# ScalarE takes norms and guards, GpSimd five head outputs, in the opening of a two-layer block

## The reference

```
q, k, v = split(norm(x) @ W_qkv.T);  q, k = elu(q) + 1, elu(k) + 1
att = q * cumsum(k * v) / (q * cumsum(k) + 1e-9)          # cumulative over the sequence, per channel
x = x + norm(att @ W_out.T * c)
gate, up = split(norm(x) @ T(w_gate_up).T)                # T: ternary in groups of 64, times mean |w|
h = silu(gate) * up
x = x + norm(rms_norm(h) @ T(w_proj).T)
```

## Time and profile before

| | us |
|---|---|
| median of 3 runs | 1160.17 (1159.6 to 1161.37) |
| the profiled execution | 1160.26 |
| its span, first to last instruction | 1158.4 |
| PE busy | 1098.9 |
| DVE busy | 772.9 |
| POOL busy | 534.2 |
| ACT busy | 442.3 |

### The profile page before, as it was taken

One profiled execution on the slowest core, in us unless ns is written; L12 is line 12 of the kernel. 1 busy time (PEld: TensorE's weight loads), 2 busy tenths in 40 slices (PEclk: granted clock), 3 DMA queues, 4 the chain that ended last, 5 costly groups with the idle time before them and its releaser, 6 DMA issues. The chain is left out here.

```text
span 1158.4 us, 14626 instructions
## 1 busy us (share of the span) xinstructions
PE 1098.9 (95%) x5376; PEld 659.5 (57%) x5376; DVE 772.9 (67%) x1224; ACT 442.3 (38%) x752; POOL 534.2 (46%) x493
## 2 busy tenths in 40 slices
PE   6997779998999999999999999999999999899997
PEld 5886355554566864468544774458644684454443
DVE  5999988985668687438872588527863488435323
ACT  3443546665522133422443234431444134333432
POOL 2548789977344343415434254415334253224323
PEclk9998889999999999999999999999999999899999
DMA  7021234200030210002100210002100010100001
GB/s 253 29 73 37 79 88 143 74 29 1 1 109 1 73 37 1 1 1 73 37 1 1 74 37 1 1 1 73 37 1 1 16 58 1 37 1 1 37 1 37
DMA packets 29079, 44.98 MB, mean 39 GB/s; under 512 B 1360, under 2 KB 9552, under 8 KB 29008
## 3 DMA queue, kind: packets, MB, share of 16 engines
q1 hardware_dynamic: 29008, 44.05, 11.7%
HBM read 34.60 MB, written 9.44 MB: 38 GB/s over the span
## 5 line engine op out<-in xcount | busy, mean ns | idle before, releaser
L540 PE MATMUL bank<-x3t,wgu_t 128*128 128x512 f16 x1536 | 351.1, 382 | 11.2 <-ACT ht L946 9.0
L540 PEld LDWEIGHTS bank<-x3t,wgu_t 128*128 128x128 bf16 x1536 | 149.1, 99 | 194.8 <-ACT ht L946 13.9
L1235 POOL TENSOR_TENSOR acc<-acc,ht 128x512 f32<-128x512 f32 x90 | 114.6, 1274 | 270.5 <-ACT ht L987 270.3
L576 PE MATMUL bank<-wproj_t,hid 128*128 128x512 bf16 x872 | 204.8, 380 | 3.3 <-ACT wproj_t L866 3.3
L1594 DVE TENSOR_TENSOR ht<-ht,bank 128x512 f32<-128x512 f32 x112 | 76.1, 679 | 159.8 <-PE bank L540 127.3
L521 PE MATMUL bank<-xnt,wqkv_hi 128*128 128x512 f32 x672 | 168.1, 392 | 0.0
L576 PEld LDWEIGHTS bank<-wproj_t,hid 128*128 128x128 f16 x872 | 85.2, 98 | 104.3 <-issue 4.5
L521 PEld LDWEIGHTS bank<-xnt,wqkv_hi 128*128 128x128 f32 x672 | 125.1, 188 | 26.0 <-issue 0.4
L1600 DVE TENSOR_TENSOR hid<-ht,hid 128x512 f16<-128x512 f32 x109 | 90.6, 831 | 66.3 <-ACT hid L974 66.3
L974 ACT ACTIVATE hid<-ht 128x512 f16<-128x512 f32 x109 | 68.5, 629 | 160.7 <-DVE ht L1594 160.7
L1181 POOL TENSOR_TENSOR tk<-tq,ts 128x512 f32<-128x512 f32 x28 | 55.0, 1965 | 136.6 <-DVE ts L1509 112.7
(11 more groups left out here) (178 smaller groups left out, 1558.2 us busy)
## 6 DMA issues: line engine op xcount, KB each, us to landing
raw_q<-in_L_ffn_w_gate_up_dram SPq DMA_DIRECT2D x32, 256.0 KB, 2.8
xn<-in_L_attn_x_dram SPq DMA_DIRECT2D x7, 1024.0 KB, 5.1
out_dram<-xn SPq DMA_DIRECT2D x7, 1024.0 KB, 8.8
x<-in_L_attn_x_dram SPq DMA_DIRECT2D x6, 1024.0 KB, 6.6
raw_q<-in_L_ffn_w_proj_dram SPq DMA_DIRECT2D x16, 256.0 KB, 2.9
raw_a<-in_L_attn_W_qkv_dram SPq DMA_DIRECT2D x4, 768.0 KB, 8.1
xn<-in_L_attn_x_dram SPq DMA_DIRECT2D x4, 256.0 KB, 3.2
raw_out<-in_L_attn_W_out_dram SPq DMA_DIRECT2D x1, 1024.0 KB, 9.7
```

Of the source, the lines that this page charges most:

```text
L540: last = pe.matmul(bank[:], wgu_t[:, k, first_row:first_row + P], x[:, part, k], start=(n == 0), stop=(n == 2 * KD - 1))
L576: last = pe.matmul(bank[:], hid_of(f, part, k)[:, t * P:(t + 1) * P], wproj_t[:, k], start=(k == 0 and part == 0), stop=(k == MT - 1 and p ...
L1235: pool.tensor_tensor(acc[:], acc[:], ht_of(f)[:, m % 2], ALU.add).then_inc(q["acc_done"], 1)
```

## The change

- **Norms and guard.** `norm_tile(0, ..)`, `norm_tile(1, ..)`, `finish_x1_tile` and `norm_x1_tile` of chunks 0 and 1 (4 tiles each) and `den_guard` of chunks 0 and 1 (8) go from POOL to ACT, as ACTIVATE Identity with pointer bias and, for norms, pointer scale. A column `eps_att` is added for the guard.
- **Head outputs.** `back_output` and `back_lo` of (0, 0), (0, 1), (0, 2), (0, 3), (1, 0) go from DVE to POOL. Those of (1, 1) to (1, 3) stay on DVE, with a wait for the one before.
- **Loads.** W_qkv and W_out come in 16 DMAs of 256 KB, eight before the wait for chunk 0's transposes and eight behind chunk 1's x, each with its own semaphore. The load of chunk 2's x goes one half earlier.
- **Squares.** `hidden_square` of m = 0 waits for `h_done` only, in all chunks; `hidden_gate` of m = 2 waits for `h_lo` of tile 0.
- **`SUMMED = 24`.** For batches from `SUMMED` on, DVE would add the parts again (`whole`) and PE would transpose the sum alone. There are 24 batches.
- **Orders.** The `start()` lists of PE, ACT, POOL and DVE are written anew.

```diff
-                if i < KD:
-                    rows = w_qkv.rearrange("(s j p) k -> p j s k", s=3, p=P)[:, i]
+                if r < NG:
+                    j, part = divmod(r, 3)
+                    rows = w_qkv[part * D + j * P:part * D + (j + 1) * P, :]
...
+                sp.dma_start(raw_a[j][:, part], rows).then_inc(raw_a_in[r], 16)
...
-            load_raw(0)
-            load_raw(1)
-            load_raw(2)
+            for r in range(0, 8):
+                load_raw(r)
             sp.wait_ge(t1_done, KD)
             sp.dma_start(xn[:], x_ch[1]).then_inc(x_loaded, 16)
-            load_raw(3)
-            load_raw(4)
+            for r in range(8, 16):
+                load_raw(r)
...
                 elif m == 2:
                     act.wait_ge(q["sq_done"], at(MT, c, 0))
-                    if f < 2:
-                        act.wait_ge(q["h_lo"], 1)
+                    act.wait_ge(q["h_lo"], at(MT, c, 0))
...
-                if f < 2 and m == 0:
-                    act.wait_ge(q["h_done"], 1)
+                if m == 0:
+                    act.wait_ge(q["h_done"], at(MT, c, 0))
                 else:
                     act.wait_ge(q["h_lo"], at(MT, c, m))
...
+            def norm_tile(c, *tiles):
+
+                for t in tiles:
+                    if t == 0:
+                        act.wait_ge(LN["1"]["nb_s"], c + 1)
+                    act.activation(xn[:, t], xn[:, t], ACT.Identity, bias=LN["1"]["nb"][:, t:t + 1],
+                                   scale=LN["1"]["rstd"][:, t:t + 1]).then_inc(xn1_ready, 1)
+
+            def den_guard(s, j):
+
+                tk = sets_of(s)[1][:, j % 2]
+                act.wait_ge(den_mul, at(KD, s, j))
+                act.activation(tk, tk, ACT.Identity, bias=eps_att[:, 0:1]).then_inc(den_ready, 1)
...
+            def back_output(s, j):
+
+                tq, tk, tr, ts = sets_of(s)
+                d = j % 2
+                pool.wait_ge(num_ready, at(KD, s, j))
+                pool.wait_ge(rec_done, at(KD, s, j))
+                pool.wait_ge(carry_done, 2 * KD * s + 2 * (j + 1))
+                pool.tensor_tensor(tr[:, d], tq[:, d], tk[:, d], ALU.mult).then_inc(att_out, 1)
```

More of the change, by code:

```diff
@@ L202, in sandwich_kernel @@
         RAW = 3
+        SUMMED = 24
         PARTS = 1
@@ L222, in sandwich_kernel @@
         setup_done = sem("setup_done")
-        raw_a_in = [sem(f"raw_a_in{i}") for i in range(KD + 1)]
+        raw_a_in = [sem(f"raw_a_in{r}") for r in range(4 * KD)]
         raw_q_in = [sem(f"raw_q_in{i}") for i in range(RAW)]
@@ L237, in sandwich_kernel @@
         q_diff = sem("q_diff")
+        q_whole = sem("q_whole")
         q_t = sem("q_t")
@@ new lines, in start @@
+                cast_half(11, 0, 1), finish_x1_tile(1, 0), hidden_gate(1, 4), put_half(6, 0), cast_half(12, 0)
+                finish_x1_tile(1, 1, 2), put_half(6, 1), hidden_square(1, 3), finish_x1_tile(1, 3), turn(6), cast_half(12, 1)
+                put_half(7, 0, 1), turn(7), cast_half(13, 0), hidden_gate(1, 5), hidden_hi(1, 4), put_half(8, 0)
+                norm_x1_tile(1, 0, 1, 2, 3), cast_half(13, 1), put_half(8, 1), x3_hi_of(1, 0, 1, 2, 3), cast_half(14, 0)
+                hidden_hi(1, 5), cast_half(14, 1), hidden_square(1, 4), hidden_gate(1, 6), hidden_square(1, 5), put_half(9, 0)
@@ L1074, in _ @@
+                split_x(3, 0, 1, 2, 3)
             start()
@@ L1396, in diff, with whole @@
                     dve.tensor_tensor(yq[:], yq[:], wb[:], ALU.subtract).then_inc(q_diff, 1)
+            def whole(*batches):
+                for b in batches:
+                    wb, yq = PLACES[b]
+                    dve.wait_ge(q_diff, b + 1)
+                    dve.tensor_tensor(yq[:], yq[:], wb[:], ALU.add).then_inc(q_whole, 1)
             def stats(which, c, src, wait):
@@ L1715, in start @@
-                scale_max(3), front_products(1, 2), scale_row(3), scale_rec(3), scale_bound(1), scale_sums(4), clip(2)
-                back_output(1, 1), diff(1), round_off(2), sum_keys(1, 2), back_lo(1, 1), x3_lo_of(0, 0, 1, 2, 3), row_shrink(1)
-                scale_max(4), scale_sums(5), feature_k(1, 3), sum_values(1, 2), diff(2), scale_rec(4), scale_max(5), carry_key(1, 2)
-                carry_value(1, 2), scale_rec(5), scale_sums(6, 7), hidden_value(0, 0), back_reciprocal(1, 2), clip(3)
@@ L1719, in start @@
-                feature_q(1, 3), clip(4), round_off(3), hidden_lo(0, 0), front_products(1, 3), hidden_value(0, 1), sum_keys(1, 3)
-                sum_values(1, 3), diff(3), round_off(4), carry_key(1, 3), carry_value(1, 3), scale_row(4), scale_max(6)
-                scale_rec(6), scale_row(5), scale_bound(2), clip(5), scale_max(7), scale_rec(7), back_reciprocal(1, 3)
-                back_output(1, 2), back_output(1, 3), back_lo(1, 2), hidden_lo(0, 1), back_lo(1, 3), round_off(5), clip(6)
-                hidden_value(0, 2), scale_sums(8), round_off(6), scale_max(8), hidden_value(0, 3), hidden_lo(0, 2), scale_rec(8)
@@ new lines, in start @@
+                back_reciprocal(1, 3), back_output(1, 3), back_lo(1, 2), diff(4), back_lo(1, 3), hidden_lo(0, 0), clip(5)
+                hidden_lo(0, 1), clip(6), round_off(5, 6), scale_sums(7), scale_max(7), scale_sums(8), scale_rec(7)
+                hidden_value(0, 2), scale_max(8), scale_sums(9), scale_row(6), diff(5), stats_tile("2", 1, 0, 1), scale_max(9)
+                scale_row(7), scale_bound(3), hidden_lo(0, 2), scale_rec(8), clip(7), stats_tile("2", 1, 2), diff(6), row_shrink(2)
```

345 lines of the change are left out of this document (166 added, 179 removed).

## The result

The changed kernel takes 1143.26 us in the median of four executions (1140.78 to 1145.12), against 1159.88 us of the kernel before on the same chip: a ratio of 0.9855, with an interval of 0.9836 to 0.9875, so 14.5 to 19.0 us faster. Forecast were 1148.5 us, in a range of 1142.0 to 1156.5. The direction was right, the mechanism mostly, and the gain came out 5 us larger than forecast.

What follows compares the result with a forecast made beforehand. VectorE was taken as the bound in the middle stretch (99.5 to 180 us), GpSimd close behind, ScalarE with room. Terms 0 - 8.5 - 3.3 = -11.8 us from 1160.3 gave 1148.5 us, range 1142 to 1156.5.

Steps and rivals of the forecast that it cites:

- The opening (0 us): Up to 58 us: PE starts 1.6 to 1.9 us sooner, given back at chunk 1's late split; bounds -1.9 and +2.
- `diff(0)` at 98.5: VectorE from 58 us to the first weight transpose: `diff(0)` begins at 98.5 instead of 102.30, 3.8 us sooner.
- 98 to 142 us (6.9): Chunk 1's attention projection starts near 133, not 141.93: 8.9 us, less 2 for stretched VectorE instructions.
- the copy behind it (1.6): Behind 142 us: half of PE's 3.2 us wait for `put_half` behind `turn(4)` goes, 1.6 us.
- part 3: 98 to 142 us and the copy behind: earlier `diff(0)`, GpSimd relief and new order give 8.5 us; bounds 3.0, 20.9.
- (b): Rival: stall chain dissolves further, less idle keeps the clock up; two thirds of 20.9 us plus 3.3; 1143, 11%.
- Which I leave: Behind 180 us: PE's 3.3 us wait for `wproj_t` taken as unchanged, costed at nothing.
- The later steps (3.3): Five later steps with attention: the first square's dropped wait saves 0.67 us each, 3.3 us; bounds 0 and 9.0.
- (a): Rival: only the removed VectorE work counts, stretched instructions and queues eat the rest; 6.3 us, 1154, 17%.
- (c): Rival, slower: ScalarE becomes the gate, decided once PE's waits for its copies pass some 20 us; 1164, 7%.
- (d): Rival: gain until 142 us lost in new waits before 300, last steps keep their waits; 1160, 5%.
- The rule on the two sides of SBUF: VectorE with both inputs in SBUF and GpSimd reading SBUF exclude each other; new products might cost 14 us, removals free more.

Runs made afterwards that it cites:

- loads_back: Changed kernel with the five large weight loads (768 and 1024 KB) again in place of 256 KB transfers: 1142.58 us, ratio 0.9855.
- loads_alone: Kernel before with only its attention weights in 256 KB transfers, each with its own semaphore: 1159.65 us, ratio 1.0006.
- heads_back: Changed kernel with the five head outputs and their low parts back on VectorE: 1148.59 us, ratio 0.9904.
- norms_back: Changed kernel with norms of chunks 0 and 1, both x1 finishes and x1 norms back on GpSimd, guards still on ScalarE: 1149.41 us, ratio 0.9916.
- old_orders: Changed kernel with all moved work kept, but all four engine orders as in the kernel before, moved calls placed where operands are ready: 1166.82 us, ratio 1.0067.
- squares_alone: Kernel before with only the new wait of the first square: 1156.02 us, ratio 0.9971.
- orders_alone: Changed kernel's orders with nothing moved; loads, squares, norms, guards and heads as in the kernel before: 1162.49 us, ratio 1.0031.
- put_first: Changed kernel with `put_half(0, 0)` ahead of the norms of x1 on ScalarE: 1140.86 us, ratio 0.9839.
- put_more: Changed kernel with three ScalarE copies, `put_half(0, 0)`, `put_half(0, 1)` and `put_half(1, 1)`, taken ahead of other work: 1141.41 us, ratio 0.9846.

## Why the prediction came out as it did

**The opening (0 us): right.** PE starts sooner, by 2.9 us in these two profiles (9.87 to 6.93; 7.7 in the second), and keeps nothing of it: `loads_back` and `loads_alone` both come out level. The last split of chunk 1 ended at 56.4 us (57.8 forecast), and the group that waits for it began at 56.5 or, in the second profile, at 58.3. Up to here one execution differs from another by more than the term.

**`diff(0)` at 98.5: 96.95.** From chunk 1's first group to the first half transpose it is 41.2 us in both profiles of the change against 44.8: 3.5 us, forecast 3.8. `heads_back` shows that the ten instructions taken from DVE are behind it: with them back, this distance is 45.0.

**98 to 142 us (6.9) and the copy behind it (1.6): right in place, and in size right or up to 1.9 us short.** From the half transpose to the attention projection of chunk 1 it was 38.9 us and is 34.0 in one profile, 35.7 in the other. With the 3.5, which the 6.9 contain, that is 8.5 or 6.8 us. From there to the first gate unit of chunk 1 it was 43.6 and is 41.6 or 41.4, some 2 us where 1.6 were forecast. The sum is 10.4 or 8.9 us, forecast 8.5. The relief of GpSimd, which I did not price, is as large a piece as any (`norms_back`: 7.1 us in all, 4.4 to 5.9 of it in this stretch, 122.7 us long there). Of the three things that part 3 adds up, the third, the order, failed as a gain of its own: alone it costs 3.6 us. Yet without it the moves cost 7.8, as I placed them in `old_orders`: each needs the other.

**What part 3 leaves out: the clock.** Part 3 moves start times by DVE's queue and takes all that is won as idle time of PE: its bound is all of the 20.9 us, its sign an idle time near 13. PE's side of the stretch has two entries. Idle time fell by 7.2 us (6.1 in the second profile, 14.8 us left), and 3.2 us (2.8) more went as busy time for the same matmuls, since less of the stretch ran at the lower of the two levels, 1.2 GHz. The earlier trace rows had it in plain sight: a granted clock of 0.82, 0.73 and 0.87 in 64.5 us. I used that in rival (b) only, without a figure. The two entries aren't two separate gains: where PE waits for DVE, quicker matmuls alone would only lengthen the wait, and DVE's own 11.1 us (9.9) less cover the whole of the stretch's gain. How much shorter the stretch would be had the clock stayed at 0.91, no run shows.

**"Which I leave": the 3.3 us behind 180.** Here the clock was overlooked too. In the kernel before, PE stands 3.30 us for `wproj_t` at 277 us, and the granted clock over 270 to 290 us is 0.91:

```profile
277.03 2.92 PE L576 MATMUL bank<-wproj_t,hid 128*128 128x512 bf16 x8 [3.30 <-ACT wproj_t L866]
```

```profile
270.00:290.00 20.00, 16.70 (x95) 8.12 (x93) 10.39 (x17) 10.29 (x18) 14.30 (x14) 0.91 0.00 1
```

In the changed kernel it is two waits of 1.08 us, and the clock of the same work is 1.00:

```profile
267.75 3.40 PE L582 MATMUL bank<-wproj_t,hid 128*128 128x512 bf16 x15 [1.08 <-ACT wproj_t L873]
```

```profile
258.00:276.00 18.00, 16.92 (x112) 8.83 (x111) 8.57 (x14) 8.56 (x15) 15.71 (x13) 1.00 0.01 1
```

In the second profile the two waits are 0.87 each. Behind the wait of 3.3 us the granted clock falls to the lower level in all four kernels whose trace has it (before, `squares_alone`, `loads_alone`, `old_orders`), and at this place in none of the ten traces with the two short waits. So 1.1 to 1.6 us of this wait go, less a new one of 0.4 us for a copy, and the matmuls take 1.3 us less; with small change it is the 2.5 us measured. It comes from the new order, which I had taken as showing only where it makes a wait. `orders_alone` has this stretch at 127.6 us, 1.7 of the 2.5, and `norms_back` the same, so the last 0.8 need the norms on ACT. `old_orders` has 129.1 with the 3.30 us wait unchanged, `loads_alone` and `squares_alone` 129.3 like the kernel before.

**The later steps (3.3): right.** 3.5 us undone, 3.4 alone. Five waits of the ten are left with 6.1 us in all (forecast 5.5).

Together: 8.9 to 10.4, 2.5 and 3.5 make 14.9 to 16.4 us where the ratio gives 16.8 and the forecast had 11.8. The first stretch was sized nearly right, 0.4 to 1.9 us short. The 5 us that the forecast lacks are this, the 2.5 of the second stretch, which had no term and is half clock, and 0.4 to 1.9 us that lie outside these stretches or are the chance by which two profiles of one program differ.

**The rivals.** (a), only the removed work, falls: 1154, and `norms_back` and `heads_back` show 12.8 us for two parts. (b) has the measured time, 1143, but its way there was two thirds of the idle time in the middle stretch, and about one third went. The clock, which it names, did rise, but 2.5 us came from a stretch that (b) doesn't speak of: that its figure is met is in part luck. (c) falls: PE waits 11.6 us for ACT's copies out of bank 3 where it waited 13.2 (the 8.5 of the prediction is the first of three lines), far from the 20 at which it would decide. `norms_back` shows that some 5 of the 11.6 are the norms' doing. They aren't simply to be had back: `put_first` and `put_more` bring the first line of these waits from 11.3 to 8.6 and 7.8 us, other waits come in their place, and the time falls by 2 us at most. (d) falls.

**The rule on the two sides of SBUF** (the Trainium skill, SBUF - State Buffer, "SBUF: two separate sides") was weighed as an argument against the change. The traces agree with it: `diff`, with both operands in SBUF, ends behind the GpSimd operation of two tensors in 8 of 8 cases before and in `old_orders`, while `hidden_value`, with one operand in a bank, isn't lengthened in any of 32 and 31. The trace of before could have shown this already, where the prediction says that it doesn't show which instruction locked. The page names as locked both an operation of two SBUF inputs, as `diff` is, and one in a mode that takes both ports; that the roundings, 0.41 us for as many columns as `diff` does in 0.68, run in such a mode is a reading, not shown. In the changed kernel the ten new GpSimd operations were no such loss: the lengthening in the stretch fell, by the estimate above, from 8 us to 5.5 or 6.6.

## What to carry to other kernels

First count the work of the engine that bounds the stretch: here DVE had 10 to 11 us less to do, and the stretch became 9 to 10 us shorter. Where the granted clock of a stretch is below 1, put a term in the sum for it: here some 4 us of PE's busy time went with 7 or 8 of idle time. Ask of each wait that one leaves alone whether a new order splits it: behind a wait of 3.3 us the clock fell here, behind two of 1.1 it did not. And judge moved work and its order together: either alone made this kernel slower, by 3.6 us and, in the one placement that was run, 7.8 us, both together 16.8 us faster.

## What the runs showed of the hardware

- An ACTIVATE with Identity over 128x512 floats in SBUF takes 0.71 or 0.72 us with a bias column and 0.81 us with scale and bias columns, against 0.63 us for the plain copy of the earlier trace rows.
- Between the exponentials it cost no table load: the trace has six loads at SiLU's line, five at the exponential's and one at the start, before and after.
- A DVE TENSOR_TENSOR of two SBUF operands that begins during a GpSimd TENSOR_TENSOR ends some 0.55 us behind it, a bf16 TENSOR_SCALAR within SBUF some 0.28 us: 0.68 us became 1.68, 0.41 became 1.48 and 1.54. The product of `hidden_value`, with one operand in a bank of PSUM, keeps its time (0 of 32 lengthened), and so does the 1.2 us reduction of `scale_sums` (0 of 11).
- With transfers of 256 KB PE began at 6.7 to 8.2 us in ten traces, with 768 KB at 8.7 to 9.9 in four, at 0.5 us of SyncE per issue. Two profiles of one program differ by 1.8 us at 58 us (56.5 and 58.3).
- The clock fell to 1.2 GHz behind PE's single wait of 3.30 us (20 us around it at 0.91: eight matmuls of 128x512 in 2.92 us instead of 1.89), and stood at 1.00 around two waits of 0.87 to 1.08 us.
